# Moving the output projection's additions from VectorE to ScalarE and GpSimd, in the stage that counts edges

## The reference, cut to what matters

```python
edge_index = jnp.stack([src, dst])
xn = _layernorm(x, axis=-1)
x = x + _L0_gnn_ref(xn, edge_index, L0_gnn_W, L0_gnn_b) + _L0_mix_ref(xn[None], L0_mix_W_qkv, ...)[0]
...
# in _L0_mix_ref, the end of the attention: the output projection
normed = (out - mu) / jnp.sqrt(var + EPS) * gamma + beta
return normed @ W_out + b_out
...
# in _L0_gnn_ref: one sum over all edges, per node
msg = norm[:, None] * h[col]
out = jax.ops.segment_sum(msg, row, num_segments=num_nodes)
```

## Time and profile before

| | us |
|---|---|
| median of 3 runs | 2211.28 (2209.93 to 2212.87) |
| span of the profiled execution, first to last instruction | 2207.7 |
| median less this span | 3.6 |
| PE busy in the span | 2068.7 |
| DVE busy | 1234.6 |
| ACT busy | 725.6 |
| POOL busy | 1003.1 |

### The profile page before, as it was taken

How to read it: one execution, slowest core, us unless ns; L and a number is a source line. 1 busy time by engine, 2 the same in 40 slices (tenths; PEclk the granted TensorE clock), 3 DMA queues, 4 the chain that set the end, 5 groups by cost and what they waited for, 6 DMA issues and landing times.

```text
span 2207.7 us, 41128 instructions
## 1 busy us (share of the span) xinstructions
PE 2068.7 (94%) x16448; PEld 1423.1 (64%) x16448; DVE 1234.6 (56%) x2250; ACT 725.6 (33%) x1080; POOL 1003.1 (45%) x783
## 2 busy tenths in 40 slices
PE   7989999999998999969999999999999998977997
PEld 6555564474457977734545577747877887865765
DVE  6784555547566699965534622546555633374332
ACT  5243444435563354320230512312222220052332
POOL 3218777878773200025503873049334422333554
PEclk9999999999999999979999999999999999987999
DMA  4302333324156311060001021211211212376886
GB/s 160 89 20 56 87 91 74 91 69 104 23 140 158 113 54 39 13 200 20 20 0 47 28 73 38 88 39 34 66 41 40 55 29 63 140 304 180 153 153 106
DMA packets 128120, 182.14 MB, mean 83 GB/s; under 512 B 52066, under 2 KB 97257, under 8 KB 121679
## 3 DMA queue, kind: packets, MB, share of 16 engines
q1 hardware_dynamic: 111102, 150.87, 22.6%
q0 software_dynamic: 16848, 28.90, 7.8%
HBM read 120.82 MB, written 53.49 MB: 79 GB/s over the span
## 4 chain that ended last, share of the span: by engine, by line
PE 76%; POOL 9%; DVE 6%; issue 5%; DMA 2%; ACT 1%; SPq 0%; DVEq 0%; POOLq 0%; ACTq 0%
PE ps L494 19%; PE ps L497 19%; PE ps L496 19%; POOL edges_sorted L1532 4%; PE pt L717 2%; DVE RB L798 2%; PE ps L699 2%; PE pt L912 2%; PE pt L479 1%; POOL WR L1524 1%; POOL WR L1523 1%; POOL WR L1520 1%; PE pt L1155 1%; PE ps L1174 1%; PE ps L1175 1%
## 5 line engine op out<-in xcount | busy, mean ns | idle before, releaser
L494 PE MATMUL ps<-WR,RB 128*128 128x256 f16 (+2 forms) x2248 | 630.2, 280 | 6.9 <-DVE SR L1817 3.5
L496 PE MATMUL ps<-WR,RB 128*128 128x256 f16 (+2 forms) x2248 | 629.8, 280 | 0.0
L497 PE MATMUL ps<-WR,RB 128*128 128x256 f16 (+2 forms) x2248 | 629.7, 280 | 0.0
L494 PEld LDWEIGHTS ps<-WR,RB 128*128 128x128 f16 x2248 | 220.2, 98 | 52.7 <-DVE RB L446 3.1
L494 PE MATMUL ps<-RB,WR 128*128 128x512 f16 (+1 forms) x720 | 246.5, 342 | 8.0 <-DVE RB L446 7.4
L1532 POOL DMA_INDIRECT edges_sorted<-SR x160 | 199.9, 1250 | 117.4 <-DVE SR L1922 56.9
L497 PEld LDWEIGHTS ps<-WR,RB 128*128 128x128 f16 x2248 | 220.0, 98 | 42.5 <-issue 0.7
L497 PE MATMUL ps<-RB,WR 128*128 128x512 f16 (+1 forms) x720 | 246.4, 342 | 0.0
L496 PE MATMUL ps<-RB,WR 128*128 128x512 f16 (+1 forms) x720 | 246.4, 342 | 0.0
L496 PEld LDWEIGHTS ps<-WR,RB 128*128 128x128 f16 x2248 | 220.5, 98 | 39.7 <-issue 0.8
L1473 POOL TENSOR_TENSOR WR<-WR,units 128x3072 f32<-128x3072 f32 (+2 forms) x16 | 74.2, 4635 | 371.5 <-PE ps L494 317.3
(11 more groups left out here) (348 smaller groups left out, 4041.9 us busy)
## 6 DMA issues: line engine op xcount, KB each, us to landing
WR<-in_w_moe SPq DMA_DIRECT2D x64, 256.0 KB, 3.6
moe_split<-WR SPq DMA_DIRECT2D x128, 128.0 KB, 1.8
RB<-moe_split SPq DMA_DIRECT2D x8, 2048.0 KB, 15.6
WR<-in_w_mix SPq DMA_DIRECT2D x12, 1024.0 KB
WR<-in_w_mix SPq DMA_DIRECT2D x8, 1536.0 KB
RB<-in_x SPq DMA_DIRECT2D x18, 512.0 KB, 6.1
WR<-in_w_out SPq DMA_DIRECT2D x8, 1024.0 KB
RB<-counts SPq DMA_DIRECT2D x10, 640.0 KB, 4.8
```

Source lines behind the costliest of these rows:

```text
L494: m = nc.tensor.matmul(o, ah, bh, start=(k == 0), stop=False)
L496: nc.tensor.matmul(o, ah, bl, start=False, stop=False)
L497: m = nc.tensor.matmul(o, al, bh, start=False, stop=(k == n - 1))
```

## The change

The addition leaves VectorE. ScalarE copies a unit's product, scaled, from PSUM into one of two buffers `gtmp` and frees the bank; GpSimd adds the buffer to X. ScalarE waits with unit u for GpSimd's addition of unit u-2, by the new semaphore `part_added`. `evac` is now raised by ScalarE. The waits for the node rows' second load (`xr_loaded`) move to GpSimd. Nothing else moves, and the values computed are the same.

```diff
@@ -340,6 +340,7 @@
+        part_added = sem("part_added")
@@ -1278,6 +1279,12 @@
                 if st >= 4:
                     act.wait_ge(b_free, st - 3)
                 nc.scalar.activation(rw[st % 4], pb[st % 3][0:TN, 0:BW], ACT.Copy).then_inc(rows_out, 1)
+                if st in OUTS_AT:
+                    u = OUTS_AT.index(st)
+                    act.wait_ge(mm_done, TILE0["mix0_out"] + u + 1)
+                    if u >= 2:
+                        act.wait_ge(part_added, u - 1)
+                    nc.scalar.activation(gtmp[u % 2], out_bank(u), ACT.Copy, scale=1.0 / (OS0 * WS)).then_inc(evac, 1)
                 if st - 1 in (OUTS_AT[0], OUTS_AT[NT], OUTS_AT[2 * NT]):
                     weights_high(act, 17 + OUTS_AT.index(st - 1) // NT)
@@ -1555,6 +1562,13 @@
             g.memset(Bc[:, NT:NB].rearrange("p a b -> p (a b)").bitcast(F32), 0.0).then_inc(bc_clear, 1)
+            for u in range(4 * NT):
+                if u < NT:
+                    pool.wait_ge(xr_loaded[u], 32)
+                pool.wait_ge(evac, TILE0["mix0_out"] + u + 1)
+                x = X[:, u % NT, u // NT * 256:u // NT * 256 + 256]
+                g.tensor_tensor(x, x, gtmp[u % 2], ALU.add).then_inc(part_added, 1)
+            pool.wait_ge(part_added, 4 * NT)
             pool.wait_ge(deg_ready, 1)
@@ -2007,13 +2021,6 @@
             for st in range(NST):
                 if st % 2 == 0 and st // 2 + 2 < NST // 2:
                     hot(st // 2 + 2)
-                if st in OUTS_AT:
-                    u = OUTS_AT.index(st)
-                    if u < NT:
-                        dve.wait_ge(xr_loaded[u], 32)
-                    dve.wait_ge(mm_done, TILE0["mix0_out"] + u + 1)
-                    x = X[:, u % NT, u // NT * 256:u // NT * 256 + 256]
-                    stt(x, out_bank(u), 1.0 / (OS0 * WS), x, ALU.mult, ALU.add).then_inc(evac, 1)
                 add_rows(st)
```

## The result

Over 20 runs each, the changed kernel has a median of 2213.93 us (2211.5 to 2217.66) and the kernel before 2209.08 us (2206.79 to 2212.87). The ratio is 1.0021, with an interval of 1.0015 to 1.0027: slower by 4.6 us, 3.3 to 6.0 by the interval. The two medians differ by 4.85 us. The direction was as forecast; the forecast was +10.1. The span of the profiled execution is 2212.0 us against 2207.7.

What follows compares the result with a forecast made beforehand. TensorE, then VectorE, bounds the stage, both full. VectorE's 160.2 + 6.6 + 40 x 0.46 = 185.2 us against 175.1 gives +10.1; span 2207.7 + 10.1 = 2217.8, plus 3.6 to the median, 2221.4 us; range 2210.5 to 2231.

Steps and rivals of the forecast that it cites:

- The terms 2.86, 0.03, 0.33 and 2.20: VectorE's us in the stage: a supertile pair without a unit; extra for an odd-place unit, an even-place unit, a weights' low half.
- the 1.7 given as the most: Stage without GpSimd's additions: TensorE limits, so the time is that of the kernel before or up to 1.7 us less.
- d = 0.46: Stall of VectorE for each of GpSimd's 40 additions in the stage: 0.46 us, lower end 0.20, upper 0.73.
- an estimated 0.73 us: Length of one GpSimd addition of 128 by 256: 0.54 us for 256 numbers on top of a fixed 0.186.
- The duration less a fixed 0.26: One form of VectorE's stall for a GpSimd addition: 0.73 - 0.26 = 0.47 us.
- 0.04 for the gap: Mean part of a stall that costs nothing, from VectorE's 0.20 us idle behind a pair's first row addition.
- the stall that grows with size: Other form of VectorE's stall: the part of GpSimd's addition that grows with size, 0.54 us for 256 numbers.
- the forecast's own case: Stage slowed by stalls of d from 0.32 to 0.6 us per GpSimd addition: 2215.7 to 2227 us, chance 0.60.
- the wider range: Whole kernel's time from the no-change time at which TensorE limits, 2210.5, up nearly to the whole-instruction case, 2231 us.
- Hidden stalls: GpSimd's additions fall where VectorE would stand still anyway; d under 0.32, not under 2209.5 us, chance 0.22.
- whole-instruction stalls: Each GpSimd addition holds VectorE for its whole length or more: d = 0.73, +20.9 us, 2232.2 us, chance 0.12.
- a relief that counts all: TensorE not really full, so VectorE's 7.2 us less work counts and no stall matters: 2204 us, chance 0.06.

Runs made afterwards that it cites:

- a kernel that had not been thought of then: Kernel before, additions still on VectorE, with the 40 units spread over supertiles 1 to 111, all odd: 2200.75 us against 2209.37, ratio 0.9956.
- the mixed places: Kernel before with the 40 units spread evenly over supertiles 1 to 111, 22 at odd and 18 at even ones: 2206.02 us against 2208.66, ratio 0.9985.
- The half-width run: Changed kernel with GpSimd's additions taking 128 of the 256 columns: 2208.41 us against 2208.28 for the kernel before, ratio 0.9996.

## Why the prediction was right in kind and too high in size

**What bounds the kernel: right.** Both engines are full, VectorE with 1.1 us to spare. The terms 2.86, 0.03, 0.33 and 2.20 gave 168.0 for a kernel that had not been thought of then, and 167.6 was measured; for the mixed places they gave 173.4, and 172.4 was measured.

**The removal buys next to nothing: right.** Without GpSimd's additions the gain was 1.2 us, of the 1.7 given as the most, and its interval includes none.

**ScalarE's copies cost nothing: right.** They take 0.384 us each, and the same run shows no loss.

**GpSimd's addition: this is the term that was mis-sized.** The prediction charged VectorE d = 0.46 us for each addition and the runs show 0.34 to 0.355; most of that comes from the length of the addition itself. The prediction put "an estimated 0.73 us" on it, by a straight line through the rows of 512 and 1024 numbers. It takes 0.65. The four sizes measured are 0.41 (the least), 0.65, 1.27 and 2.35 us for 128, 256, 512 and 1024 numbers, and no one straight line goes through them.

**The stall: right in form.** "The duration less a fixed 0.26" and 0.04 for the gap, with 0.65 put in, gives 0.35; measured were 0.34 by the distance and 0.355 by the lengthened instructions. Then 40 x 0.35 - 8.3 = +5.7 us, against +5.4 in the distance. Of the error of 4.7 us in the distance, 40 x 0.08 = 3.2 is the addition's duration. The other 1.5 is in what I had added to the fixed form when I went from 0.43 to 0.46, towards the stall that grows with size (1.2 us), and in rounding. The half-width run speaks against that form: it would give 0.27 for 128 numbers, and single stalls were 0.16 and 0.22. The fixed 0.26 taken from one instruction held for the comparisons (0.25); on the first comparison it is 0.2. The medians differ by 4.85 us and not by 5.4; that last half microsecond is not explained, and it is as small as what single executions differ by.

**The forecast's interval.** d = 0.34 lies within the 0.32 to 0.6 of the forecast's own case, near its edge. The time of 2213.9 lies below that case's 2215.7 to 2227 and within the wider range, which goes down to 2210.5. The range was drawn around a median of three runs, 2211.3, which stood 2.2 us above the median of 20; a difference is what was to be forecast, and it came out at a little under half of it. The 3.6 us between median and span are also not all start and end of the launch: every timed run lies 1.7 to 1.8 us above its own span, and the rest is that the profiled execution was quicker than the median of three. Both slips shift the absolute time and leave the difference alone.

**The rivals.** Hidden stalls, whole-instruction stalls and a relief that counts all fell. As a price, the whole instruction would be 0.65 each and +17.7 us; the trace says 0.34. The rule of the Trainium skill in "SBUF — State Buffer" ("Who interferes with whom"), that the one who issues first holds the other for the whole instruction, is right here about who is held and too dear as a price; the measurement decides.

**What would show it.** The distance between pairs with a unit near 3.3 us, the stalls near 40 in number, and TensorE's waits came as written. The last row addition began at 967.3 and not near 972 (961.4 before). Some of GpSimd's additions lasted longer than the 1.1 us expected, as below. That an addition meets an instruction "each time and holds the next" was right in number, 40 of 40, but the one held isn't always the next: GpSimd was seen to wait through a whole first comparison (line 1977 above) and then to hold the ones behind it.

## What to carry to other kernels

When two engines are both full, take work from one only if the work's new place does not reach back: an addition of 0.65 us on an idle GpSimd cost VectorE 0.35 us, more than the 0.18 (mean of 0.03 and 0.33) that VectorE had paid for doing it itself. Cost an instruction by the distance between repeats in the timeline with and without it, not by its duration: 0.42 us of addition was worth 0.03 where it stood in a gap. And look for the better place of the work before its better engine: one line that put the same additions into the gaps, and spread them, gained 8.6 us.

## What the runs showed that I had not expected

A GpSimd instruction that only writes SBUF held the comparisons with one tensor input (78.1 us against 71.8) and left every instruction with two SBUF inputs at its usual length. The Trainium skill says so for the second kind in "SBUF — State Buffer" ("Who interferes with whom"), that such a VectorE instruction contends with a GpSimd instruction that reads SBUF and not with one that only writes; this case's trace agrees, 482 and 685 ns with and without 40 memsets.

GpSimd waits too. Three additions of 0.65 us last 1.9 to 3.7, and each of them was asked for while VectorE was at a weights' low half of 2.28 us (line 604):

```profile
788.89 2.28 DVE L604 SCALAR_TENSOR_TENSOR WR<-WR 128x2048 f16<-128x2048 f32 x1
```

```profile
789.40 3.27 POOL L1570 TENSOR_TENSOR RB<-RB,SR 128x256 f32<-128x256 f32 x1 [2.94 <-ACT SR L1287]
```

This one did not get in when the low half ended at 791.17 either, but waited through the row addition and the first comparison behind it; the four comparisons of 792.09 were then held, spanning 2.02 us, by this addition and the next. The waiting itself cost nothing here, as nobody needed the sum before the stage's end.

A wait on the semaphore that ends another engine's gap does not place work in the gap, but right behind it, which was the dearest of the places tried (0.41 us each against 0.35).
